# Expert tiles of 512 rows that scale their rows by the share and scatter them by token, in a vision tower of five stages

## The reference

```python
h = tok(x)                                   # patches, softmax attention over all 3136 tokens, projection
h = h + attn(layernorm(h))                   # gated linear attention: running sums over the tokens
h = h + experts(layernorm(h))
h = h + l1_attention(layernorm(h))           # linear attention, 12 heads, q and k divided by column sums
h = h + bit_ffn(layernorm(h))                # weights rounded to -1, 0, 1; activations to 8 bits

def experts(x):
    routing = softmax(gelu(x @ w1 + b1) @ w2 + b2)          # 8 experts
    topv, topi = top_k(routing, 2)
    sparse = one_hot(topi) * topv; sparse /= sum(sparse) + 1e-8
    z = gelu(x @ down_w[e] + down_b[e])                     # 192 -> 256, for each expert e
    return layernorm(x + sum_e sparse[e] * (z @ up_w[e])) * gamma + beta
```

## Time and profile before

| | |
|---|---|
| median of 3 runs | 2704.89 us (2699.2 to 2707.6) |
| the profiled execution's own time | 2725.97 us |
| its span | 2724.0 us, 45853 instructions |
| PE busy | 2317.9 us (85%) |
| DVE busy | 1979.0 us (73%) |
| ACT busy | 1535.6 us (56%) |
| POOL busy | 1023.4 us (38%) |
| packets, bytes by DMA | 69145, 162.82 MB |

### The profile page before, as it was taken

The page is one execution under the profiler, slowest core; times in us unless marked ns, Lnnn a source line. Parts: engine busy times, 40 slices in busy tenths (PEclk is TensorE's granted clock), DMA queues, the critical chain, the costliest instruction groups (busy, mean ns, idle before and its releaser), DMA issues. The chain is left out here.

```text
span 2724.0 us, 45853 instructions
## 1 busy us (share of the span) xinstructions
PE 2317.9 (85%) x14046; PEld 1685.0 (62%) x14047; DVE 1979.0 (73%) x5187; ACT 1535.6 (56%) x2777; POOL 1023.4 (38%) x1108
## 2 busy tenths in 40 slices
PE   8999999999996999999964999944687787577776
PEld 4444444444443888888854999944576777345554
DVE  5777777777773899999963444437788976899997
ACT  2444444444444778888753556535665652577777
POOL 1100100100000166566672444458877840344444
PEclk9999999999997999999976999977687878688788
DMA  2000000000002011111125777741111100000001
GB/s 58 0 18 13 0 18 13 0 9 1 0 0 91 8 52 52 50 52 50 52 82 183 254 254 258 254 134 51 48 44 45 50 25 9 25 26 26 26 26 31
DMA packets 69145, 162.82 MB, mean 60 GB/s; under 512 B 12977, under 2 KB 32342, under 8 KB 68702
## 3 DMA queue, kind: packets, MB, share of 16 engines
q1 hardware_dynamic: 39426, 94.27, 10.6%
q0 software_dynamic: 21504, 44.99, 5.8%
q10 hardware_dynamic: 8064, 21.68, 2.6%
HBM read 63.98 MB, written 63.88 MB: 47 GB/s over the span
## 5 line engine op out<-in xcount | busy, mean ns | idle before, releaser
L211 ACT ACTIVATE prob<-pscore 128x896 f32<-128x896 f32 x336 | 308.0, 917 | 423.3 <-PE pscore L293 423.3
L418 DVE TENSOR_REDUCE pmax<-ppre 112x1 f32<-112x512 f32 x656 | 424.5, 686 | 162.5 <-PE ppre L260 162.4
L307 PE MATMUL pout<-prob,xkey 128*64 128x448 f32 x1344 | 328.3, 567 | 0.4 <-ACT prob L211 0.4
L260 PE MATMUL ppre<-xh,yh 49*112 49x512 f32 x656 | 291.4, 446 | 7.8 <-DVE pmax L418 4.1
L723 POOL DMA_INDIRECT rows_in<-xr,idx x224 | 242.7, 1083 | 131.5 <-DVE idx L1249 73.8
L193 POOL CAST yh<-ynext 113x448 fp32r<-113x448 f32 x28 | 17.2, 614 | 667.9 <-DVE pmax L418 639.8
L260 PEld LDWEIGHTS ppre<-xh,yh 49*112 49x112 f32 x656 | 112.8, 172 | 239.8 <-issue 103.5
L1708 POOL DMA_INDIRECT yg<-rows_out,place x224 | 231.1, 1032 | 62.4 <-issue 62.2
L293 PE MATMUL pscore<-yh,xh 49*128 49x448 f32 x700 | 241.6, 422 | 0.4 <-DVE yh L438 0.4
L1558 POOL TENSOR_TENSOR zl<-z,zh 128x448 fp32r<-128x448 f32 x126 | 144.3, 1146 | 220.1 <-ACT zh L1524 210.6
L2222 POOL TENSOR_TENSOR yg<-y,gout 112x512 f32<-112x512 f32 x112 | 142.9, 1282 | 188.3 <-DVE y L2495 185.3
(11 more groups left out here) (384 smaller groups left out, 6627.2 us busy)
## 6 DMA issues: line engine op xcount, KB each, us to landing
wd<-down SPq DMA_DIRECT2D x63, 512.0 KB, 3.0
xb<-rows_in SPq DMA_DIRECT2D x63, 448.0 KB, 3.6
rows_out<-yb ACTq DMA_DIRECT2D x63, 336.0 KB, 3.2
out<-ho SPq DMA_DIRECT2D x28, 336.0 KB, 2.8
rows_in<-zero SPq DMA_DIRECT2D x15, 448.0 KB
rows_in<-xr,idx POOLq DMA_INDIRECT x224
yg<-rows_out,place POOLq DMA_INDIRECT x224
xkey<-in_xkey SPq DMA_DIRECT2D x4, 800.0 KB, 6.5
```

The lines of the kernel that those rows point to most:

```text
L211: nc.scalar.activation(prob[j % 3][:, :, :], pscore[j % 2][:, :, 0:CH], ACT.Exp).then_inc(exped, 1)
L260: pe.matmul(out[:, :], yh1[rows, q * T:(q + 1) * T], xh[b % 2][rows, block * 512:(block + 1) * 512], start=True, stop=True, tile_position= ...
L307: mm = pe.matmul(pout[i * LO:(i + 1) * LO, 0:CH], xkey[b % 2][:, 2 * j + i, :], prob[j % 3][:, i, :], start=(j == 0), stop=(i == 1 and j = ...
L418: nc.vector.reduce_max(pmax[:, q, 2 * block + half:2 * block + half + 1], bank(u, depth), AX.X).then_inc(pre_max, 1)
```

## The change

1. **Mixer.** The last slot is split by queries: each half of the array takes 224 of the 448 (HC = CH // 2), with the same 128 keys. For that the 64 last keys of the first half are loaded to the second half too, by one more small DMA for each image.
2. **Route stage.** A row of rows_in gets 260 floats: the first gate, the second gate, the second expert's number and twice the token's number are behind the 256. share writes the first three into xr instead of keeping the gates in an array of their own. POOL's scatter waits for share_out too, computes the token column and replaces the second gate by its difference from the first. The regions and the fills are in units of TR = 512 rows; the rows for filling come from the host.
3. **Tile stage.** 56 tiles of 512 rows (128 partitions by 4). DVE makes zl in place of POOL, reads from each row which of the two experts this is (take_dest) and so the share and the destination, and scales y by the share in four operations. POOL scatters y by token with four indirect DMAs of 128 rows for each tile. The store by ACT goes.
4. **Linear stage.** As rows_out now is in the order of the tokens, SP loads the rows of a chunk by one plain DMA; the eight gathers go. add_experts is two additions of 112x768. The normalisation xn is four activations and a copy in place of eight activations. The weights of the FFN are loaded and rounded at this stage's start.
5. **FFN stage.** The load and the rounding of the weights go from its start.

The diff, cut to its core:

```diff
+TR = 512
+RW = 260
+REGION = TOK * B + TR
+NTILE = 2 * TOK * B // TR + E - 1
...
@@ mixer_phase: slot_scores and slot_pv
-                    for i in (1 - half, half) if j < SLOTS - 1 else (0,):
+                    for i in (1 - half, half):
                         rows = slice(i * LO, i * LO + X1)
-                        mm = pe.matmul(pscore[j % 2][:, i, 0:CH], x[b % 2][rows, keys], y[rows], start=(n == 0),
-                                       stop=(n == 2), tile_position=(i * LO, 0))
+                        queries = slice(0, CH) if j < SLOTS - 1 else slice(i * HC, (i + 1) * HC)
+                        mm = pe.matmul(pscore[j % 2][:, i, 0:queries.stop - queries.start], x[b % 2][rows, keys],
+                                       y[rows, queries], start=(n == 0), stop=(n == 2), tile_position=(i * LO, 0))
...
-                    mm = pe.matmul(pout[0:LO, 0:CH], xkey[b % 2][:, 2 * j, :], prob[j % 3][:, 0, :],
-                                   start=False, stop=True, tile_position=(0, 0))
+                    for i in range(2):
+                        mm = pe.matmul(pout[i * LO:(i + 1) * LO, i * HC:(i + 1) * HC], xkey[b % 2][:, 2 * j, :],
+                                       prob[j % 3][:, i, 0:HC], start=False, stop=True, tile_position=(0, i * LO))
...
@@ attend_route_phase, POOL: scatter
                 if 0 in tiles:
+                    pool.wait_ge(R["xr_ready"], r + 1)
...
+                    nc.gpsimd.tensor_scalar(xr[r % G3][:, :, 259], twice[:], 1.0, float(2 * CH * r), ALU.mult,
+                                            ALU.add).then_inc(R["twice_out"], 1)
                     pool.wait_ge(R["idx_out"], r + 1)
+                    pool.wait_ge(R["share_out"], r + 1)
+                    rows = xr[r % G3]
+                    nc.gpsimd.tensor_tensor(rows[:, :, 257], rows[:, :, 257], rows[:, :, 256], ALU.subtract).then_inc(
+                        R["twice_out"], 1)
+                    pool.wait_ge(R["twice_out"], 2 * r + 2)
...
@@ attend_route_phase, DVE: share
-                link(nc.vector.tensor_tensor(gate[:, r * TPC:(r + 1) * TPC, :], top[:, :, 0:2],
-                                             both[:].broadcast_to([T, TPC, 2]), ALU.mult))
+                dve.wait_ge(R["xr_ready"], r + 1)
+                nc.vector.tensor_copy(xr[r % G3][:, :, 258], which[:, :, 1])
+                nc.vector.tensor_tensor(xr[r % G3][:, :, 256:258], top[:, :, 0:2], both[:].broadcast_to([T, TPC, 2]),
+                                        ALU.mult).then_inc(R["share_out"], 1)
+                dve.wait_ge(R["share_out"], r + 1)
...
@@ tile_phase, POOL
-                    nc.gpsimd.tensor_tensor(zl[i][m][:], z[m][:], zh[i][m][:].bitcast(F32),
-                                            ALU.subtract).then_inc(S["zl_out"], 1)
...
+            def scatter(t, j):
+
+                pool.wait_ge(S["half_out"], 2 * t + 2)
+                for q in range(TPC):
+                    pool.wait_ge(S["y_out"], 4 * t + q + 1)
+                    nc.gpsimd.indirect_dma_start(
+                        rows_out, bass.IndirectOffsetOnAxis(ap=dest[j][:, q:q + 1], axis=0),
+                        yb[j % 2][:, q, :], None).then_inc(y_store[j % 2], 16)
...
+            for i in range(2):
+                pool.wait_ge(y_store[i], 16 * TPC * (NTILE // 2))
...
@@ tile_phase, DVE
+            def take_dest(t, j, n):
+
+                if after(t, 4):
+                    dve.wait_ge(y_store[j % 2], 16 * TPC * (n - 1))
+                if after(t, 1):
+                    dve.wait_ge(S["half_out"], 2 * t)
+                x = xb[j % 2]
+                e = owner[:, bass.ds(t, 1)]
+                nc.vector.scalar_tensor_tensor(second[:], x[:, :, 258], e, x[:, :, 257], ALU.is_equal, ALU.mult)
+                nc.vector.scalar_tensor_tensor(first[:], x[:, :, 258], e, x[:, :, 259], ALU.is_equal,
+                                               ALU.add).then_inc(S["half_out"], 1)
+                dve.wait_ge(S["half_out"], 2 * t + 1)
+                nc.vector.tensor_tensor(share[j][:], second[:], x[:, :, 256], ALU.add)
+                nc.vector.scalar_tensor_tensor(dest[j][:], x[:, :, 258], -1.0 - j % 2, first[:], ALU.mult,
+                                               ALU.max).then_inc(S["half_out"], 1)
+
+            def low_z(t, i, m):
+                dve.wait_ge(S["z_out"], 2 * t + m + 1)
+                nc.vector.tensor_tensor(zl[i][m][:], z[m][:], zh[i][m][:].bitcast(F32),
+                                        ALU.subtract).then_inc(S["zl_out"], 1)
+
+            def take_y(t, j, n):
+
+                if after(t, 2):
+                    dve.wait_ge(y_store[j % 2], 16 * TPC * n)
+                dve.wait_ge(S["half_out"], 2 * t + 2)
+                for q in range(TPC):
+                    dve.wait_ge(S["up_mm"], 2 * t + q // 2 + 1)
+                    nc.vector.tensor_scalar(yb[j % 2][:, q, :], py[j % 2][:, q // 2, (q % 2) * D:(q % 2 + 1) * D],
+                                            share[j][:, q:q + 1], None, ALU.mult).then_inc(S["y_out"], 1)
...
                 if not last:
                     take_low(t + 1, 1 - i)
...
+                    take_dest(t + 1, (j + 1) % 4, n + i)
+                low_z(t, i, 0)
+                low_z(t, i, 1)
+                if after(t, 1):
+                    take_y(t - 1, (j - 1) % 4, n + i - 1)
...
@@ linear_attention_phase, SP
+            def load_rows(g):
+                if g >= 2:
+                    sp.wait_ge(S["acc_out"], g - 1)
+                sp.dma_start(yg[g % 2][:].rearrange("p q k d -> p q (k d)"),
+                             rows_out[g * 2 * CH:(g + 1) * 2 * CH].rearrange("(q p k) d -> p q (k d)", q=TPC, p=T)
+                             ).then_inc(loaded[g % 2], 16)
+
+            sp.dma_start(win[:], ins["win5"]).then_inc(S["f_in"], 16)
+            sp.dma_start(wout[:], ins["wout5"]).then_inc(S["f_in"], 16)
...
@@ linear_attention_phase, POOL
-                if here(s + 4):
-                    gather_rows(s + 4, (0, 1, 2))
                 if here(s + 3):
                     factor(s + 3)
-                if here(s + 4):
-                    gather_rows(s + 4, (3,))
                 if here(s + 2):
                     factor4(s + 2)
...
@@ linear_attention_phase, DVE
+                nc.vector.tensor_tensor(rows, rows, yg[g % 2][:, :, 0, :], ALU.add).then_inc(S["half_out"], 1)
+                dve.wait_ge(S["half_out"], g + 1)
+                nc.vector.tensor_tensor(rows, rows, yg[g % 2][:, :, 1, :], ALU.add).then_inc(S["acc_out"], 1)
...
             split_weights()
+            quantised_weights()
             dve.wait_ge(S["e_in"], 32)
```

More of the change, by code:

```diff
@@ L551, in _, with attend_route_phase @@
             inverse_root(nc, dve, link, rstd[:], var[:], root[:], dif[:])
[L554 to L555 removed]
+def attend_route_phase(nc, ins, h, bns, mean, rstd, minus, eye, held, tile_e, tile_f, tile_r, down, rows_in,
+                       scattered):
     M = 64
@@ L1495, in tile @@
                 down_product(t, i, n)
-                if not isinstance(t, int) or t > 0:
+                if after(t, 1):
                     up(t - 1, 1 - i)
+            pe.wait_ge(S["one_out"], 1)
+            pe.matmul(pz[0][:, 0:64], one[:], tile_f[:], start=True, stop=True).then_inc(S["e_mm"], 1)
             front(0, 0, 0)
+            pe.wait_ge(S["e_out"], 1)
             tiles(pe, tile)
@@ L1742, in _ @@
             pe.wait_ge(S["w_in"], 16 * NW)
-            pe.wait_ge(S["w_ready"], 4)
+            pe.wait_ge(S["w_ready"], 5)
+            pe.wait_ge(S["f_sums"], 2)
+            for i in range(2):
+                mm = pe.matmul(pqk[i][:, 0:1], ones[:], wsum[:, i:i + 1], start=True, stop=True)
+            mm.then_inc(S["f_mm"], 1)
             def transposes(g):
```

369 lines of the change are left out of this document (161 added, 208 removed).

## The result

The changed kernel takes 2834.32 us (median, 2822.23 to 2838.25), the kernel before 2704.68 us in the same measurement: slower, ratio 1.0484 with a 95% interval of 1.0444 to 1.0523, or +129.6 us. These are four executions; a fifth took 2844.96 us. The profiled execution is the shortest of them, 2822.23 us with a span of 2820.3. The forecast was 2873 within 2785 to 2955; sign and mechanism held, and the sum was 39 us too high.

A forecast was written before the change was run, and what follows sets the result against it. No single engine was taken to bound the kernel: TensorE fills the mixer and tile stages, three engines the route stage, and the linear stage waits. Terms −14+205+5+8+16−41−10.5 = +168.5 on the 2704.89 us median gave 2873 us, range 2785 to 2955.

The forecast's parts named there:

- The route stage: Route: scatters wait for share and delay factor and add_out, +205 (148 to 275), plus +5 at the stage's end.
- The wait itself: Route, steady: add_out starts 5.9 us later in each of 25 chunks, +148.
- The clock's part: Route: PE's clock falls after each pause, w/2 = 3.5 us a chunk, a third put on DVE's waits, taken as 2.3.
- the rival in which the clock doesn't matter: Route: only the pause is lost, +148, total 2816 us; chance 22%.
- that of the long low clock: Route: the clock stays low for most of a chunk, 11 us a chunk, 275, total 2943 us; chance 14%.
- The stage's end: Route end: the last four chunks of scatters cannot begin before share either, +5 us (0 to 10).
- The other side's rival: Route: DVE's other work before add_out absorbs the stall, so the route costs 0, total 2668 us; chance 8%.
- The mixer: Mixer: the split last slot ends sooner, 0.5 us for each of 28 chunks, −14 (−17 to −8).
- The tile stage: Tiles: 56 of 6.0 us, +8 (0 to +47); tile end: last scatters, landing and POOL's drain, +16 (+5 to +22).
- the rival in which POOL bounds the tiles: Tiles: each DVE subtraction stops an issue for its full length, tile 6.7 us, +47, total 2912 us; chance 10%.
- The linear stage: Linear: start −4, first seven chunks −16, later three images −7 each; together −41 (−60 to −20).
- The FFN stage: FFN start: PE no longer waits for the weights' sums and rounding, −10.5 us (−12 to −9).

The follow-up runs named there:

- a1_factor_first: The changed kernel with POOL's route-stage order turned, so that factor comes ahead of scatter (0,1): 2642.81 us, ratio 0.9769.
- a3_wait_in_before: The kernel before with one thing added, POOL's scatter (0,1) waiting for share: 2902.17 us, ratio 1.0728.
- b2_compact_first: The kernel before with compact(), DVE's table of places, moved from the third tile to ahead of the first: 2699.53 us, ratio 0.9976.
- c6_sums_later: a1_factor_first with the weights' rounding spread, rows of chunks 0 and 1 loaded ahead of the weights, and both sums a chunk later: 2629.88 us, ratio 0.97.
- c1_zl_on_pool: a1_factor_first with the tile stage's subtraction zl back on POOL, ahead of the previous tile's scatters: 2737.68 us, ratio 1.012.

## Why the prediction was right, and where it was off

**The route stage** was forecast at 205+5 and lost 192 us by the times of the changed kernel and a1_factor_first, 195 by a3_wait_in_before and 200 by the table. The wait itself came as worked out: 5.9 us a chunk forecast, 5.76 measured, 142 us in all against 148. The clock's part was forecast at 2.3 a chunk and was 2.2 (55.0/25). That it came so near is partly luck: of w/2 = 3.5 the forecast put a third aside without a row for it. What takes it off is that part of the low time, some 1.3 and 3.5 us of 7 in turn, lies inside PE's own pause. So neither the rival in which the clock doesn't matter nor that of the long low clock held. The stage's end took 3 us (200.2 between the stages less 197.1 between the add_outs), forecast 5. The other side's rival, a stall absorbed by DVE's other work, is excluded by the total of DVE's wait.

**The mixer**: −14 forecast, −17.1 measured, the end of the range. It is 0.61 a chunk where I had taken 0.5. PE's idle time ahead of a chunk fell from 0.70 to 0.33 us, and PE now starts right behind yh (434.43 and 434.46), so yh's chain is what is left, as forecast. Where the other 0.24 us of the 0.61 come from was not looked into.

**The tile stage** was the term that was most in error: +8 for the tiles and +16 for the end, and the stage grew by 6 to 10 us (363.2 to 365.2 against 355.3 to 356.9). The end was right: from PE's drain to the block's end it is 21.1 us now (1956.0 to 1977.1), and was 5.7 (1800.8 to 1806.5), 15 more. (The 3 us for a landing were an estimate that no row showed; the drain began 1.6 us behind the end of the last issue, at 1966.1.) The tiles themselves gave back 5 to 9. Two steps of the sum were wrong. I took a tile of 6.0 us, for POOL's sake; PE sets it at 5.82, which is 56×5.82 = 326, and POOL with 5.06 us of issues a tile is hardly held up by DVE: the mean issue took 0.996 us and none over 1.5. So the rival in which POOL bounds the tiles did not hold. The rival had each of DVE's subtractions stop an issue for its whole length, as for the one long operation in the earlier trace rows; the measurement says that these short ones rarely do. The Trainium skill, SBUF — State Buffer, in its box on the "DVE blocks DMA" trap, says that GpSimd cannot write descriptors while DVE runs an operation in a 2-port mode, and names a copy as one; no run here shows the mode of an operation, and the box does not speak of subtractions. And "63×5.20" was one even tile times 63; the stage before also had compact's stop, which b2_compact_first shows to be worth 6.5 us. Its removal stood in the diff, and the prediction costed it at nothing without naming it. Up products with 128 columns follow each other after 111 ns ((1804.51−1801.85)/24), near the 112 of my ratio. The Trainium skill, TensorE: Matmul & The Clock Gate, section LDWEIGHTS, gives a load's time as columns/1.2 ns, by which the estimate was 107; the measured 111 decides.

**The linear stage**: −41 forecast, −47 to −49 in the profiles of the three kernels with 451 to 453 us and −60 in the changed kernel's own. The start was undersized: the third chunk's factor comes 39.4 us behind the block's start (1977.1 to 2016.52) where it came 48.5 behind it (1806.5 to 1855.04), −9 and not −4. So the gathers' going gave the next chunks more than the weights took from the first. The first seven chunks came nearly as taken, 11.3 each (2016.52 to 2095.41), −18 and not −16. The seven of a later image were 106.3 us,

```profile
2017.56 0.21 POOL L1715 TENSOR_TENSOR veps<-agg,eps 112x4 f32<-112x4 f32 x1
...
2123.85 0.81 POOL L1715 TENSOR_TENSOR veps<-agg,eps 112x4 f32<-112x4 f32 x1 [0.28 <-DVE agg L1975]
```

and are 99.7 in a1_factor_first, the −7 of the forecast, and 96.2 in the changed kernel's own profile, which is what sets its 440 apart; why two executions of one code differ so is open. c6_sums_later shows what the start still costs: some 13 us are to be had by moving rounding and loads out of DVE's way, so that about as much as the FFN stage gained was paid here.

**The FFN stage**: −10.5 forecast, −13.3 in the table (408.5 against 421.8). PE begins 8.9 us after its block does in place of 20.5; what is over lies in the stage and was not tested.

**The sum**: with −17 for the mixer, 192 to 195 for the route, +8 for the tiles and their end, −47 for the linear and −13 for the FFN stage the sum is +123 to +126, beside 129.6 measured. Of the 39 us that the forecast was too high, 16 are the tile term, 15 to 18 the route and its end, 6 the linear stage and 3 each the mixer and the FFN. (These make 43 to 46; the terms miss the measured total by 4 to 7, which stays open.) That the profile of before was slow in its route stage did no harm, since the sum was made of differences; carried to the profiled execution itself the forecast, 2894.5, is 72 us above the 2822.23 measured.

## What to carry to other kernels

Before an indirect DMA's data gets one more producer, write down what stands behind the DMA in its queue: here the wait was for a 0.2 us operation, and what it held up was another engine's critical input, four issues later. The remedy cost nothing, an order of four lines in the issuing engine, and made a slower kernel the faster one. Where a stage's price is computed from one repeated unit, count the units' total against the stage's length first; the difference is an operation that nobody costed.

## What the runs showed of the hardware

A pause of PE of 2.9 us cost more by the clock (2.6 us a chunk) than one of 5.4 us (2.2), since a long pause has part of the low time inside itself; one of 1.7 us lowered the clock in some chunks, for some 3.4 us, and not in others.

POOL's drain at the end of a block took 9.19 to 9.63 us in all blocks in which it had issued indirect DMAs, even where the last one had been issued 24.6 us earlier (before, linear stage: last start 2224.1, drain at 2248.7, 9.62 us), and 0.04 to 1.24 us in those without. It is about half of the tile stage's longer end.

An indirect DMA costs POOL 1.26 us of its own time for 128 rows of 768 bytes, and nothing of it overlaps POOL's arithmetic (c1_zl_on_pool). A DVE subtraction of 0.69 us from SBUF (zl, two for four issues) lengthened such an issue by 0.04 us in the mean and by 0.5 at most, where one of 2.29 us had added 2.0.
